# Image four's chain moved ahead of image three's keys and of the first attention units, with three score banks and O copied in two parts

## What is computed

```
x = x + deformable_conv3x3(group_norm(x))        # 9 taps, bilinear samples as a 256 x 256 matrix per tap
t = tokens(x)                                    # 4 images x 256 tokens x 64
t = t + attention_block(layer_norm(t))           # 8 heads of 32, softmax, projection, norm, gated MLP, norm
t = t + recurrent_cell(layer_norm(t))            # 256 steps over the tokens, 4 rows (images) a step
```

## Time and profile before

| | |
|---|---|
| time, median of 3 runs | 390.86 us (390.81 to 391.2) |
| span of the profiled execution, first to last instruction | 394.5 us |
| own time of the profiled execution | not given beside its span |
| PE, DVE, ACT, POOL busy | 94%, 60%, 57%, 16% of the span |
| convolution and images' chains | to about 65 us |
| tile 0's units, image 3's chain | about 63 to 87 us |
| projection to the cell's first step | about 87 to 97.2 us |
| cell, with later tiles beside it | from 97.2 us to the end |

### The profile page before, as it was taken

One profiled execution on the slowest core, in us unless ns is written; L12 is line 12 of the kernel. 1 busy time (PEld: TensorE's weight loads), 2 busy tenths in 40 slices (PEclk: granted clock), 3 DMA queues, 4 the chain that ended last, 5 costly groups with the idle time before them and its releaser, 6 DMA issues.

```text
span 394.5 us, 15298 instructions
## 1 busy us (share of the span) xinstructions
PE 370.9 (94%) x5893; PEld 197.1 (50%) x5893; DVE 238.4 (60%) x1225; ACT 226.1 (57%) x1076; POOL 62.3 (16%) x139
## 2 busy tenths in 40 slices
PE   7999997999999999999999999999999999999996
PEld 2676663444455455545544464445455545544332
DVE  2497753235666676666566656666665766564443
ACT  2686754321775486458646854775486468634433
POOL 5001111122110211111021201110221112020000
PEclk9999999569999999999999999999999999999999
DMA  7000000000000000000000000000000000000000
GB/s 261 0 2 12 12 12 10 15 2 2 4 3 2 2 7 3 3 5 4 2 2 7 3 3 2 7 2 3 3 6 4 2 6 4 4 2 6 2 2 4
DMA packets 4806, 4.33 MB, mean 11 GB/s; under 512 B 3837, under 2 KB 4286, under 8 KB 4734
## 3 DMA queue, kind: packets, MB, share of 16 engines
q1 hardware_dynamic: 4432, 2.84, 2.5%
q10 hardware_dynamic: 302, 0.52, 0.4%
HBM read 2.57 MB, written 0.26 MB: 7 GB/s over the span
## 4 chain that ended last, share of the span: by engine, by line
PE 64%; DVE 16%; ACT 11%; issue 6%; POOL 1%; DMA 1%; ACTq 0%; DVEq 0%
PE bank L724 17%; PE bank L391 11%; PE bank L533 9%; DVE bank L1221 6%; PE bank L547 5%; DVE H L1231 5%; ACT bank L898 4%; ACT bank L891 4%; PE bank L565 4%; PE bank L458 3%; PE bank L448 2%; PE bank L419 2%; ACT E L821 2%; PE bank L634 1%; PE bank L410 1%
## 5 line engine op out<-in xcount | busy, mean ns | idle before, releaser
L391 PE MATMUL bank<-FB 128*128 128x512 bf16 (+2 forms) x497 | 142.3, 367 | 1.2 <-DVE FB L920 1.2
L724 PEld LDWEIGHTS bank<-H,VW 64*32 64x32 f32 x3072 | 52.3, 106 | 106.0 <-DVE H L1231 104.4
L891 ACT ACTIVATE bank<-bank 64x8 f32<-64x8 f32 x256 | 37.6, 147 | 89.4 <-PE bank L724 89.0
L724 PE MATMUL bank<-H,VW 64*32 64x4 f32 x3072 | 74.6, 176 | 12.8 <-DVE H L1231 2.7
L1221 DVE TENSOR_TENSOR_SCAN bank<-bank,SU 64x12 f32<-64x12 f32 x256 | 48.6, 190 | 50.1 <-ACT bank L891 47.5
L1231 DVE SCALAR_TENSOR_TENSOR H<-TO,bank 64x4 f32<-64x4 f32 x256 | 40.7, 159 | 45.2 <-ACT bank L898 35.6
L368 POOL TENSOR_SCALAR E<-E,rinv 128x256 f32<-128x256 f32 x62 | 29.9, 483 | 134.5 <-DVE rinv L1031 134.4
L391 PEld LDWEIGHTS bank<-FB 128*128 128x128 bf16 x497 | 39.0, 98 | 21.5 <-issue 2.3
L898 ACT ACTIVATE bank<-bank 64x4 f32<-64x4 f32 x256 | 38.4, 150 | 16.2 <-DVE bank L1221 0.4
L895 ACT ACTIVATE TO<-bank 64x4 f32<-64x4 f32 x256 | 43.8, 171 | 6.2
L1215 DVE SCALAR_TENSOR_TENSOR SU<-H,bank 64x4 f32<-64x4 f32 x256 | 41.3, 161 | 9.1
(11 more groups left out here) (115 smaller groups left out, 329.8 us busy)
## 6 DMA issues: line engine op xcount, KB each, us to landing
AW<-in_attn_w SPq DMA_DIRECT2D x1, 768.5 KB, 7.6
DW<-in_dcn_w SPq DMA_DIRECT2D x1, 576.0 KB, 6.2
X<-in_x_fm SPq DMA_DIRECT2D x1, 256.0 KB, 3.0
X<-in_x_fm ACTq DMA_DIRECT2D x1, 256.0 KB, 4.8
T<-T0T SPq DMA_DIRECT2D x16, 16.0 KB, 1.8
Y<-YT SPq DMA_DIRECT2D x16, 16.0 KB, 1.8
out_dram<-OUT SPq DMA_DIRECT2D x8, 32.0 KB, 1.4
CW<-in_conv_w SPq DMA_DIRECT2D x1, 243.5 KB, 3.7
```

Source lines behind the costliest of these rows:

```text
L391: nc.tensor.matmul(idle[:, 0:n], FB[:, 0:P], FB[:, 0:n], start=True, stop=True)
L724: mm = nc.tensor.matmul(gate_out(m, gate, r, slice(B * s, B * (s + 1))), VW[0:C, gate, r], H[0:C, (STEPS * m + s - 1) % RING, :], start=Fa ...
L891: nc.scalar.activation(GT[:, :, 1:3].rearrange("p b g -> p g b"), b_cell[m % 2][0:C, 0:2 * P].rearrange("p (g s b) -> p g s b", g=2, b=B)[ ...
```

## The change

1. PE's list around the end of the convolution. Image 2's `channels` and the last six gathers come first, then image 2's keys, then image 3's `tokens`, and only then units 0 and 1. Image 2's values, unit 2, image 3's `channels` and keys follow, with one 512-column fill on either side of `channels`; then the first `turn_probs`. From there the units run with `turn_probs` two and `weigh` three units behind `scores`.
2. DVE's and ACT's lists are put into the same order. On DVE image 3's `sampled` stands ahead of image 2's queries, and its stats and `token_norm` ahead of the first `rinv`. On POOL image 3's root stands ahead of the first `normalised`.
3. Scores of tile 0 use three banks, so `scores` of unit u waits for `rinv` of unit u - 3. `nmax`, `rinv` and `E` become rings of four (for all tiles).
4. DVE takes over three copies from ACT: the second halves of `V` of images 2 and 3 (`second_values`) and the second half of image 3's keys (`last_keys`). Image 3's queries go to a bank of their own and come out in one instruction.
5. `O` of tile 0 is copied in two parts: three images (`heads_early`) when unit 5 is weighed, and image 3 (`heads_last`, 32 columns a copy) after unit 7; image 3's `weigh` writes into another bank. For tile 0 both `project_turned` now stand ahead of both `project`, and the fill in front of them is gone. In the units' tail one fill between `turn_probs` and `weigh` of units 6 and 7 is gone.

The core of the diff:

```
-        b_s_first = [b_s1, b_c1]
-        b_et_first, b_pv_first = b_cs, b_c0
+        b_s_first = [b_s1, b_c1, b_et]
+        b_et_first, b_pv_first, b_pv_last = b_cs, b_c0, b_et
...
-            for b in range(B - 1):
-                first_root(b)
-            normalised(0, 0)
-            first_root(B - 1)
-            for u in range(1, NU - 2):
+            for b in range(B):
+                first_root(b)
+            for u in range(NU - 2):
                 normalised(0, u)
...
+                elif m == 0:
+                    pe.wait_ge(e_inv, i - 2)
                 else:
                     pe.wait_ge(e_inv, i - 1)
...
+            channels(2)
+            for g in range(len(GROUPS) - BATCH, len(GROUPS)):
+                gather(g)
+            keys_queries(2)
+            tokens(3)
+            scores(0, 0)
             scores(0, 1)
-            tokens(3)
+            values(2)
             scores(0, 2)
+            fill(COLS_EARLY, b_pv_first)
+            channels(3)
+            fill(COLS_EARLY, b_pv_first)
+            keys_queries(3)
             turn_probs(0, 0)
             scores(0, 3)
             turn_probs(0, 1)
             weigh(0, 0)
-            channels(3)
+            values(3)
...
+            for u in range(5, NU):
+                scores(0, u)
+                turn_probs(0, u - 2)
+                weigh(0, u - 3)
+            for u in (NU - 2, NU - 1):
                 fill(COLS_EARLY, b_x)
                 turn_probs(0, u)
-                fill(COLS_EARLY, b_x)
                 weigh(0, u - 1)
...
+            def heads_early(hg):
+                dve.wait_ge(pv_mm, NU - HG)
...
+            def heads_last(hg):
+                dve.wait_ge(pv_mm, NU)
```

More of the change, by code:

```diff
@@ L47 @@
 KEYS_AT = (4, 7, 10)
-VALUES_AT = (6, 9, 12)
+VALUES_AT = (6, 9)
 SLOTS = 2 * BATCH
 TURNS = 3
+UNIT_RING = 4
 FIRST = -9
@@ L560, in weigh @@
                     pe.wait_ge(o_done, HG * m + 1)
+                dst = b_pv if m else b_pv_last if b == B - 1 else b_pv_first
+                if m == 0 and u == NU - HG:
+                    pe.wait_ge(e_inv, NU - HG)
                 for half in range(HALVES):
@@ L568, in weigh @@
                 mm.then_inc(pv_mm, 1)
[L570 to L573, removed]
+            for j in range(len(GROUPS) // BATCH):
+                for g in range(BATCH * j, BATCH * (j + 1)):
+                    turn(g)
                 if j in TOKENS_AT:
                     tokens(TOKENS_AT.index(j))
-                if j in CHANNELS_AT:
+                if j in CHANNELS_AT[:-1]:
                     channels(CHANNELS_AT.index(j))
@@ L598, in _ @@
             weigh(0, 1)
[L599 to L610, removed]
+            for u in range(5, NU):
[3 more added lines that the diff above has]
+            for u in (NU - 2, NU - 1):
                 fill(COLS_EARLY, b_x)
                 turn_probs(0, u)
-                fill(COLS_EARLY, b_x)
                 weigh(0, u - 1)
             fill(COLS_EARLY, b_x)
-            weigh(0, 7)
+            weigh(0, NU - 1)
             def project_turned(m, hg):
                 pe.wait_ge(o_done, HG * m + hg + 1)
+                if m == 0:
+                    pe.wait_ge(o_early, HG)
                 if hg == 0 and m >= 1:
@@ L707, in beside @@
                         project_turned(m, 0)
-                        project(m, 0)
+                        (project_turned if m == 0 else project)(m, 1 if m == 0 else 0)
                     if o == PROJECT + 1:
-                        project_turned(m, 1)
+                        (project if m == 0 else project_turned)(m, 0 if m == 0 else 1)
                     if o == PROJECT + 2:
@@ L741, in _ @@
                     fill(cols, idle)
-                elif start(0) + PROJECT <= g < start(0) + CELL_READY and g not in (start(0) + PROJECT + 1, start(0) + PROJECT + 2):
+                elif start(0) + PROJECT <= g < start(0) + CELL_READY and not start(0) + PROJECT <= g <= start(0) + PROJECT + 2:
                     fill(COLS_EARLY if g < start(0) + NARROWED else MOST, b_cell[1])
@@ L804, in keys_out @@
             def keys_out(b):
-                for hg in range(HG):
+                for hg in range(HG if b < B - 1 else 1):
                     act.wait_ge(k_mm, 2 * b + hg + 1)
-                    if hg == 0:
+                    if hg == 0 and b < B - 1:
                         act.wait_ge(q_done, b + 1)
@@ L812, in values_out @@
                 act.wait_ge(v_mm, b + 1)
-                for h in range(HALVES):
+                for h in range(HALVES if b < B - 2 else 1):
                     nc.scalar.copy(V[:, b, h, :], (b_y, b_k)[h][:, 0:256]).then_inc(v_sb, 1)
@@ L849, in _ @@
                         values_out(VALUES_AT.index(j))
-                    if j - 1 in KEYS_AT:
+                    if j - 1 in KEYS_AT[:-1]:
                         keys_out(KEYS_AT.index(j - 1))
-            values_out(2)
+            keys_out(2)
+            tokens_out(3)
             exponents(0, 0)
             exponents(0, 1)
-            tokens_out(3)
+            values_out(2)
+            channels_out(3)
+            keys_out(3)
+            exponents(0, 2)
             turned(0, 0)
-            exponents(0, 2)
             turned(0, 1)
-            channels_out(3)
             exponents(0, 3)
+            values_out(3)
             turned(0, 2)
[L863 to L873, removed]
+            for u in range(4, NU):
+                exponents(0, u)
+                turned(0, u - 1)
+            turned(0, NU - 1)
             def queries_out(m):
```

126 lines of the change are left out of this document (75 added, 51 removed).

## The result

The changed kernel takes 386.87 us (386.64 to 387.44), a ratio of 0.9871 to the kernel before, 95% interval 0.9823 to 0.9920. This ratio is too good: of the four times of the kernel before that it rests on, three are 390.81 to 391.20 and one is 395.23. Against the three (mean 390.96, the changed kernel's 386.95) it is 0.990. Measured again, the changed kernel takes 387.41 against 390.91, ratio 0.9908 (0.9892 to 0.9923). So the change is worth 3.5 to 4.0 us. 388.0 was predicted (385.2 to 390.2).

The account below looks back on a forecast made before the run. PE was taken to bound the stretch to the last weigh, through idle gaps and half clock. Without the clock fall, gains of 2.3 and 0.4 us make 2.7, or 386.3 + 1.9 = 388.2; 388.0 us taken, range 385.2 to 390.2.

Parts of the forecast that it names:

- The baseline: Kernel before: clock fall worth 5.5 us in the profiled 394.5 us span; 389.0 without it, 1.9 around it.
- Rival 1: Timed runs carry the whole clock dip, so the gain is the recorded 8.2 us: 382.6 us; chance 0.07.
- Chain and gathers: Before the units: gathers end at about 62.0 instead of 65.6 us, so image 3's chain starts 3.6 us earlier.
- DVE's three copies: Three copies of about 0.4 us on DVE, placed where PE has other work; each costs 0.4 if uncovered.
- Rival 4: DVE sets the pace: units 2 to 7 each wait 0.4 us; gain 0.7, about 390.2 us; chance 0.06.
- The tail: Units 6 and 7 normalised on DVE: PE idles 1.25 us before unit 6's turn_probs (0.5 to 1.9).
- The projection: Last weigh to widening matmuls: 1.76 us instead of 2.13, a gain of 0.4 us (0 to 0.7).
- The sum: Last weigh from 81.5 to 79.2 us at full clock, 2.3, plus 0.4 in the projection: gain 2.7 us.
- The clock: PE's stretch from 62 to 90 us: granted clock stays at full, with no 0.50 anywhere.
- Rivals 2 and 3: Clock falls in the new tail (389.5 us, chance 0.12), or in front, before about 70 us (392.0 us, chance 0.07).

Follow-up runs that it names:

- before_filled: Kernel before the change with nine 512-column fills added in PE's idle gaps: 390.82 us, ratio 0.9984 to the kernel before.
- keys_first: Changed kernel with image 2's keys and queries put back ahead of the last three gathers on PE: 388.64 us.
- two_banks: Changed kernel with two score banks in tile 0 instead of three and the matching wait on rinv: 389.89 us.
- combined: Changed kernel with POOL's residual sums earlier, rinv of units 4 to 6 ahead of the next largest, no fill before unit 7's turn_probs: 387.03 us.
- sums_early: Changed kernel with POOL's two residual sums of tile 0 moved behind the normalising of units 2 and 3: 386.79 us.
- o_late: Changed kernel with all copies of O behind the last weigh: 387.68 us in one run.
- project_alternating: Changed kernel with tile 0's project_turned and project alternating again, as in the old order: 388.84 us in one run.
- no_front_fill: Changed kernel without the two fills on either side of image 3's channels: 387.63 us.

## Why the prediction was right, point by point

**The baseline, right.** The step that decided most was not a cost but a comparison: a span of 394.5 over a median of 390.86, from which the text took a fall of the clock worth 5.5 us that the timed runs lacked, a span of 389.0 without it and 1.9 us around it. Undisturbed spans are 388.6 to 389.3, the changed kernel has 385.0 for 386.78 (1.8 around it), and before_filled has 389.0. The whole recorded gain, 8.2 us, was rightly not forecast as the change of the time. Rival 1 (382.6) is out. That the 389.0 agrees to the tenth is in part luck: the fall was worth 6.0 in the stretch, not 5.5, and before_filled starts 0.26 later and has 0.28 more in the cell.

**Chain and gathers, right.** First scores 63.4 forecast, 63.46 measured; image 3's keys 66.9 and 66.95; the first `turn_probs` 67.7 and 67.91. keys_first shows that the start of the chain is what counts and two_banks that the bank which lets unit 2's scores stand ahead of image 3's `channels` carries its part. Undone, the first cost more than was expected of it (1.36 instead of 0.7 to 1.0), since it opens a second wait, and the second the upper end (1.59 of 1.0 to 1.6).

**DVE's three copies, right at nothing.** Rival 4 (0.4 a unit) is out: of units 2 to 5 only unit 4 waits, 0.30 where 0.4 stood. With `rinv` ahead of `largest` in combined it is gone, while in sums_early, without that edit, it is 0.31. No run puts the three copies back on ACT.

**The tail, mis-sized.** The term was 1.25 us of idle before unit 6's `turn_probs`, from the 1.06 us of a normalising step beside a sum. It was 0.39. Unit 7 waits 0.28 where 0.25 stood, but for DVE and not for ACT, and the 0.24 that ET of unit 0 was to cost does not appear. In all, 1.5 us of idle stand where the sum had 2.8; since the work and the small gaps took 0.6 more than it had, the last `weigh` ends at 78.5 instead of 79.2. (Part of the 0.6: image 3's queries, on a bank of their own, take 0.45 us to the next start, and image 2's 0.24.)

The row was read as a property of unit 6's step, but it is one of the meeting: where the step falls decides. In the execution on record, with PE at half clock, unit 6's step fell inside the second sum and unit 7's behind it; at full clock, before and after the change, unit 6's comes at the end of the first and unit 7's inside the second. Three times a step starts inside the second sum, at 81.77, 78.58 (before_filled) and 76.15, and each time it ends 0.14 or 0.15 us behind the sum, having taken 1.06, 0.97 and 0.98 us. That first-come rule is what the Trainium skill states ("SBUF — State Buffer", "Who interferes with whom"), and the runs agree with it (0.98 beside a running sum, 0.35 without). But the 1.9 us that the prediction worked out from it took the two sums for one block, and unit 6's step was hardly held by either (0.39).

The same error stood on the other side of the comparison. For the kernel before at full clock the prediction gave unit 6 a wait of 1.15 us, and before_filled shows 0.36. So the 0.9 us too much in the changed kernel and the 0.8 too much in the kernel before cancel: the forecast of the gain does not suffer from the mis-sized term, which is luck and not knowledge.

**The projection, mis-sized.** 0.4 us forecast, 0.68 measured: from the last `weigh` to widening it was 2.51 in before_filled and 1.83 in the changed kernel. The copies went as forecast (o_late: 0.44). What the sum lacked is that pairs cost 0.29 each instead of 0.365 (project_alternating).

**The sum.** Between before_filled and the changed kernel the start of the last `weigh`, counted from PE's last turns (57.56 and 57.43), moves from 23.28 to 20.77: 2.5 us where 2.3 stood; the projection gives 0.7 where 0.4 stood; widening to first step is 8.7 in both, as forecast. That is 3.2 us of the 4.0 by spans. Of the rest, 0.44 are the nine steps of the cell, which the prediction put at nothing ("a cell as long as before"); 0.13 of start and 0.28 of the other steps are of the kind that moves between executions of one kernel. So the change itself is worth 3.6 us, which lies between the 3.5 and the 4.0 of the two measurements, and the forecast's 2.7 was 0.9 short: 0.2 in the stretch, 0.3 in the projection and 0.44 in the cell.

**The clock, right but unproven.** It is 1.00 in the changed kernel up to 380 us in every trace here, with the front fills and without. Rivals 2 and 3 did not happen; whether the change made the fall impossible or only rarer can't be told from so few executions, since the kernel before, too, lost its clock in few. Nor can it be told whether a shorter fall lies in those nine executions of the kernel before whose spans are 390.1 to 391.1: no trace of one is on record.

## What to carry to other kernels

When the profiled execution is slower than the timed ones, find what it has that they can't have, and count a change from the others; a gain that is read off the profiled execution alone is a gain over its mishap. Where a chain of short steps goes through four engines, put its first step at the head of every list that it passes, and give the work that is to lie beside it the buffers it needs to be issued first: here the order without the third bank gave back 1.6 of the 2.5 us that the stretch had gained. Compare lengths between two landmarks, not spans, when the rest of the program moves more between executions than the edit is worth.

## What the runs showed of the hardware

The start of the program wanders by 1.2 us. The same eight fills near its beginning take 1.89 us in seven traces, 2.49 to 2.55 in three and 3.57 in two, which is 0.22 and 0.43 us a fill at the two ends, with 0.17 for the last one to drain. In the tail of the kernel before a fill takes 0.39 us at 2.4 GHz and 0.61 at 1.2, 0.22 more, so these look like the clock's two levels. That is inferred from the fills' rate: the granted clock itself reads 1.00 over these rows in every run. Here are no_front_fill, the changed kernel and two_banks:

```profile
5.89 1.89 PE L395 MATMUL bank<-FB 128*128 128x512 bf16 x8
```

```profile
5.75 2.55 PE L395 MATMUL bank<-FB 128*128 128x512 bf16 x8
```

```profile
5.93 3.57 PE L395 MATMUL bank<-FB 128*128 128x512 bf16 x8
```

Only the 3.57 (two_banks and project_alternating) moves the program: there the fills outlast PE's wait for DVE's normalised input, and the last six gathers start at 59.84 and 59.97, while the other versions of the changed kernel lie at 58.81 to 59.18.

In the profiled execution of the kernel before the clock fell to 0.50, that is 1.2 GHz, after 3.45 us in which PE was busy for 2.10; it stayed there for 17.07 us, in which PE was busy for 16.37, and rose among the fills of the tail.

The four f32 projections cost 0.36 us each in alternation and 0.29 each in pairs of one kind, at the same clock and with the same operands.

The same kernel's cell takes 0.4 us more in one execution than in another at full clock, spread over its steps (281.64 and 282.04 us for the same 246).
